# Cross-attention block with an int8-emulating FFN on one core: int8 rounding in both FFN stages, a reordered down projection, a reordered end of the input projection, and text denominators of the last two groups on TensorE

## The reference

```python
def _act_fake_quant(x, clip_factor):
    scale = sigmoid(clip_factor) * max(abs(x)) / 127
    return clip(round(x / scale), -128, 127) * scale      # one scale for the tensor
def _weight_fake_quant(w): ...                            # the same with one scale per row
x = x + xattn(layernorm(x), ctx, Wq, bq, Wk, bk, Wv, bv, Wo, bo)
xq = _act_fake_quant(layernorm(x), clip_x)
h = _act_fake_quant(silu(xq @ wq(w_gate).T) * (xq @ wq(w_up).T), clip_down)
x = x + h @ wq(w_down).T
# mask: 768 image tokens attend within three blocks of 256; 256 text tokens
# attend to all image tokens and causally to text
```

## Time and profile before

| | us |
|---|---|
| median of 3 runs | 1235.87 (1234.25 to 1235.88) |
| the profiled execution, its own time | 1234.68 |
| its span, first to last instruction | 1233.0 |

### The profile page before, as it was taken

The page is one execution under the profiler, slowest core; times in us unless marked ns, Lnnn a source line. Parts: engine busy times, 40 slices in busy tenths (PEclk is TensorE's granted clock), DMA queues, the critical chain, the costliest instruction groups (busy, mean ns, idle before and its releaser), DMA issues. The chain is left out here.

```text
span 1233.0 us, 18417 instructions
## 1 busy us (share of the span) xinstructions
PE 1070.3 (87%) x6494; PEld 704.9 (57%) x6518; DVE 793.9 (64%) x1340; ACT 518.9 (42%) x885; POOL 657.9 (53%) x359
## 2 busy tenths in 40 slices
PE   5999999999079899999999997059994999996866
PEld 4888888888056566666666653036662444443322
DVE  4666555564077577777777750219987678878975
ACT  3332222232006577667767776102221565544432
POOL 2543344553506889999999999224442121000635
PEclk8999999999558899999999999569997999998988
DMA  6987777766598968678868400585994551102485
GB/s 214 308 258 257 236 221 239 261 195 200 133 192 180 235 147 188 154 176 184 192 145 184 101 24 28 184 213 167 269 277 130 172 208 35 35 1 69 139 321 205
DMA packets 128699, 217.99 MB, mean 177 GB/s; under 512 B 29175, under 2 KB 54519, under 8 KB 127416
## 3 DMA queue, kind: packets, MB, share of 16 engines
q1 hardware_dynamic: 128632, 217.11, 62.7%
HBM read 134.76 MB, written 77.74 MB: 172 GB/s over the span
## 5 line engine op out<-in xcount | busy, mean ns | idle before, releaser
L618 ACT ACTIVATE a_probs<-a_st 128x512 f32<-128x512 f32 (+2 forms) x512 | 233.6, 535 | 128.1 <-PE a_st L733 97.7
L579 POOL TENSOR_TENSOR a_prob_sums<-a_probs 128x2048 f32<-128x2048 f32 x48 | 220.1, 4585 | 52.6 <-ACT a_probs L618 43.5
L658 DVE TENSOR_REDUCE a_max<-a_work 128x2 f32<-128x512 f32 x192 | 123.0, 684 | 59.3 <-PE a_work L704 59.1
L733 PE MATMUL a_st<-a_q_stack,a_k_stack 97*128 97x512 f32 x384 | 147.0, 426 | 8.3 <-DMA a_q_stack<-a_max_rows 4.5
L704 PE MATMUL a_work<-a_k_stack,a_q_stack 96*128 96x256 f32 x384 | 85.5, 318 | 38.8 <-DMA a_q_stack<-q_split 38.8
L709 PE MATMUL a_work<-a_k_stack,a_q_stack 96*128 96x512 f32 (+1 forms) x256 | 115.1, 464 | 0.0
L1303 POOL TENSOR_TENSOR d_out<-d_out,kept_ffn_x 128x512 f32<-128x512 f32 x32 | 49.5, 1579 | 121.9 <-DVE d_out L1340 121.9
L655 DVE CUSTOM_DVE_ANT_0 a_masked_scores<-a_work,kept_mask 128x384 f32<-128x384 f32 (+1 forms) x128 | 79.5, 621 | 53.2 <-PE a_work L709 53.0
L704 PEld LDWEIGHTS a_work<-a_k_stack,a_q_stack 96*128 96x128 f32 x384 | 69.9, 204 | 60.5 <-DMA a_q_stack<-q_split 39.5
L658 DVE TENSOR_REDUCE a_max_parts<-a_work 128x1 f32<-128x512 f32 x128 | 88.0, 688 | 25.0 <-PE a_work L709 21.1
L223 POOL TENSOR_SCALAR p_x<-p_x,p_neg_mean,p_rstd 128x512 f32<-128x512 f32 x32 | 28.1, 892 | 122.7 <-DVE p_rstd L328 122.7
(11 more groups left out here) (173 smaller groups left out, 2319.6 us busy)
## 6 DMA issues: line engine op xcount, KB each, us to landing
a_k_stack<-k_split SPq DMA_DIRECT2D x48, 512.0 KB, 8.3
a_q_stack<-q_split SPq DMA_DIRECT2D x48, 512.0 KB, 14.3
kept_ffn_x<-x_scratch SPq DMA_DIRECT2D x14, 1024.0 KB, 7.3
p_c<-in_ctx_dram SPq DMA_DIRECT2D x8, 1024.0 KB, 8.9
p_x<-in_x_dram SPq DMA_DIRECT2D x8, 1024.0 KB, 11.0
v_scratch<-p_v_stage SPq DMA_DIRECT2D x16, 512.0 KB, 9.2
k_split<-p_stage_hi SPq DMA_DIRECT2D x16, 512.0 KB, 4.1
k_split<-p_stage_lo SPq DMA_DIRECT2D x16, 512.0 KB, 5.3
```

The lines of the kernel that those rows point to most:

```text
L579: pool.tensor_tensor(PP[u % 2][:], PR[2 * c % 4][:], PR[(2 * c + 1) % 4][:], ALU.add).then_inc(paired, 1)
L618: act.activation(PR[kt % 4][:, j, 0:w], STB[:, n % NST, 0:w], ACT.Exp, scale=SCALE).then_inc(edone, 1)
L658: dve.tensor_reduce(out, src, AX.X, ALU.max).then_inc(wfree, 1)
L733: op = pe.matmul(out.rearrange("p (c t) -> p c t", t=SIT), keys, q, start=True, stop=True)
```

## The change

Four things are changed.

**Projection.** In the last two steps the four parts of `ffn_rows` stand between the four value tiles instead of the four key tiles. POOL does `quantise_ffn` of step 6 ahead of the layer norm of chunk 7. SP stores the quantised piece, and in the last step also the row scales, ahead of the query tiles.

**Attention.** In the last two groups (`i >= FOLDED`, 14 and 15) POOL folds nothing. PE multiplies the text columns of each pair by ones, and those of slots 6 and 7 straight from `PR`.

**gate_up and down, quantising.** One DVE pass multiplies by the inverse scale and writes int8 (which rounds and clips); ACT copies int8 to bf16. In `down` the int8 pieces go to one buffer `HI` of one chunk.

**down.** The loops are written out. The order of chunks is 6, 7, 2 to 5, 0, 1, so the spilled chunks are read back after the first and second. From chunk 1 on PE has the four token tiles outside and the k rows inside. The last chunk's residual is added by DVE tile by tile, and its output is stored in four pieces of 256 KB.

```diff
@@ project, SP, step()
+                def ffn_store():
+                    s.reach(sp, fq, n + 1)
+                    d = gu_q[u].rearrange("(b p j) n -> b p j n", p=FP, j=FJ)[b]
+                    sp.dma_start(d, FQ[:]).then_inc(fst, 16)
+                    sp.dma_start(d_q.rearrange("(s p) n -> s p n", p=DP)[n], DQ).then_inc(fst, 16)
                 for i in range(4):
+                    if tail and i == 2:
+                        ffn_store()
+                        if final:
+                            ffn_scales()
                     item = KEY + 2 * i if i < 2 else query(final) + 2 * (i - 2)
                     s.reach(sp, free, NB + at(n) + item + 2)
...
-                s.reach(sp, fq, n + 1)
-                d = gu_q[u].rearrange("(b p j) n -> b p j n", p=FP, j=FJ)[b]
...
+                if not tail:
+                    ffn_store()
                 if not final:
                     s.reach(sp, fst, 32 * (n + 2))
                     ffn_load(n + 1, 1 - u, b + u)
@@ project, POOL
+            quantise_ffn(NCH - 2)
             norm(1, NCH)
-            quantise_ffn(NCH - 2)
             quantise_ffn(NCH - 1)
@@ project, DVE, step(b, u, final, tail=False)
                     dve.tensor_tensor(VST[t // 2][:, t % 2, :], bank(u, VALUE + t), BV[:], ALU.add).then_inc(free, 1)
+                    if tail:
+                        ffn_rows(n, t)
...
                     staged(u, n, KEY + j, j, 0, 1, KT + j)
-                    ffn_rows(n, j)
+                    if not tail:
+                        ffn_rows(n, j)
@@ attend
+        FOLDED = NGRP - 2
...
-                if c:
+                if c and i < FOLDED:
                     text = PP[u % 2][:, :, SIT:]
...
-                pool.wait_ge(cutd, 2 * i + n + 1)
-                pool.tensor_tensor(text, text, probs, ALU.add).then_inc(folded, 1)
+                if i < FOLDED:
+                    pool.wait_ge(cutd, 2 * i + n + 1)
+                    pool.tensor_tensor(text, text, probs, ALU.add).then_inc(folded, 1)
...
+                if i >= FOLDED and not wi:
+                    op = denominators(TB, p, slice(0, wt))
                 op.then_inc(pvdone, 1)
...
                         pe.wait_ge(paired, 3 * i + kt // 2 + 1)
+                        if i >= FOLDED:
+                            denominators(TB, PP[(3 * i + kt // 2) % 2], slice(SIT, 512))
                         denominators(IB, PP[(3 * i + kt // 2) % 2], slice(0, SIT)).then_inc(iden, 1)
-                    if kt == NKT - 1:
+                    if kt == NKT - 1 and i < FOLDED:
@@ gate_up
-                act.activation(XQ[u][:], X[u][:], ACT.Copy, bias=-MAGIC).then_inc(xq, 1)
+                act.activation(XQ[u][:], XI[u][:], ACT.Copy).then_inc(xq, 1)
...
-                dve.tensor_scalar(X[u][:], X[u][:], F.ix[:, 0:1], QMAX, ALU.mult, ALU.min).then_inc(p1, 1)
-                dve.wait_ge(p1, n + 1)
-                dve.tensor_scalar(X[u][:], X[u][:], -QMAX - 1.0, MAGIC, ALU.max, ALU.add).then_inc(p2, 1)
+                dve.tensor_scalar(XI[u][:], X[u][:], F.ix[:, 0:1], None, ALU.mult).then_inc(rounded, 1)
@@ down
+ORDER = tuple(range(RES, NCH)) + tuple(range(2, RES)) + (0, 1)
+        HI = s.sb("hi", [P, IT, CH], I8)
...
+                sp.wait_ge(rounded, NG * (u + 1))
                 sp.dma_start(F.h[:, u], spill[u].rearrange("p (t q) -> p t q", t=IT)).then_inc(back[u], 16)
+            for n in range(LAST):
+                sp.wait_ge(added, TT * (n + 1))
+                sp.dma_start(rows(out, n), OUT[n % 2][:]).then_inc(stored[n % 2], 16)
+                if n + 2 < NCH:
+                    load(n + 2)
+            for t in range(TT):
+                sp.wait_ge(added, TT * LAST + t + 1)
+                sp.dma_start(rows(out, LAST)[:, t, :], OUT[1][:, t, :]).then_inc(stored[1], 16)
...
+            def quantise(n):
+                if n >= RES:
+                    dve.wait_ge(back[n - RES], 16)
+                for gi, (a, b) in enumerate(GROUPS):
+                    if n:
+                        dve.wait_ge(hq, NG * (n - 1) + gi + 1)
+                    dve.tensor_scalar(HI[:, a:b, :], F.h[:, n % RES, a:b, :], IH[:, 0:1], None, ALU.mult).then_inc(rounded, 1)
...
+                    dve.tensor_tensor(OUT[u][:, t, :], BK[:, u, t, :], F.sd[:], ALU.mult).then_inc(scaled, 1)
+                    if n == LAST:
...
+                        dve.tensor_tensor(OUT[u][:, t, :], OUT[u][:, t, :], X[u][:, t, :], ALU.add).then_inc(added, 1)
...
+            for k in range(IT):
+                for t in range(TT):
+                    tile(0, k, t)
+            for n in range(1, NCH):
+                for t in range(TT):
+                    for k in range(IT):
+                        tile(n, k, t)
```

More of the change, by code:

```diff
@@ L167, in _, with ffn_scales @@
             ffn_load(0, 0, 0)
+            def ffn_scales():
+                with nc.allow_non_contiguous_dma(reason="the scales of the rows, four to a line"):
+                    for u in range(2):
+                        sp.dma_start(gu_scales[u].rearrange("(b p j) -> p b j", p=FP, j=FJ), FS[0:FP, u::2, 0:FJ])\
+                          .then_inc(fsc, 16)
+                    sp.dma_start(d_scales.rearrange("(s p) -> p s", p=DP), FS[0:DP, :, FJ]).then_inc(fsc, 16)
             def step(b, u, tail, final):
@@ L202, in _ @@
                 sp.wait_ge(q, 16 * (NCH + 1))
-            with nc.allow_non_contiguous_dma(reason="the scales of the rows, four to a line"):
-                for u in range(2):
-                    sp.dma_start(gu_scales[u].rearrange("(b p j) -> p b j", p=FP, j=FJ), FS[0:FP, u::2, 0:FJ]).then_inc(fsc, 16)
-                sp.dma_start(d_scales.rearrange("(s p) -> p s", p=DP), FS[0:DP, :, FJ]).then_inc(fsc, 16)
             sp.wait_ge(fst, 32 * (NCH + 1))
@@ L1306, in _ @@
         @blk.scalar
         def _(act):
-            act.sem_inc(full, 2 * TT)
-            def step(n, u, slot):
-                act.wait_ge(full, TT * (n + 1))
+            for n in range(NCH):
+                if n >= 2:
+                    act.wait_ge(full, TT * (n - 1))
                 for gi, (a, b) in enumerate(GROUPS):
-                    act.wait_ge(p2, NG * n + gi + 1)
-                    act.activation(HQ[u][:, a:b, :], F.h[:, slot, a:b, :], ACT.Copy, bias=-MAGIC).then_inc(hq, 1)
```

141 lines of the change are left out of this document (59 added, 82 removed).

## The result

The changed kernel takes 1221.26 us (median of 4 runs, 1219.58 to 1222.71) against 1235.88 (1234.25 to 1236.03) beside it: ratio 0.9884, 95% interval 0.9867 to 0.9901. It is faster by 14.6 us (1.2%), not by the 35 forecast; 1221 lies above the range of 1190 to 1207.

What follows compares the result with a forecast made beforehand. It took PE to bound the projection, POOL attention, PE gate_up (first chunk exposed) and DVE down. Savings of 0 + 9.8 + 1.2 + 24.0 = 35.0 us from 1234.68 gave 1199.7 us, range 1190 to 1207.

Steps and rivals of the forecast that it cites:

- The wait put into step 6: Projection: DVE waits for the weight piece until 254.9, PE is held 5.8 us, then 2.4 lost to slow clock.
- Nothing else in step 6 comes too late: Projection: beyond that wait nothing is late; POOL's rounding runs from 261 to 275, step 6 is 8.2 us later in all.
- In step 7 PE does not wait: Projection: DVE waits again, but PE wants its bank at about 296.3 and value tile 1 frees it at 295.9.
- The end of the stage: Projection: ends at 326.4 to 326.8 against 326.3, term 0; query stores landing behind the scales add under 6.0 us.
- the 0.5 that the forecast itself allowed: Projection: POOL's last rounding ends at 312.5 instead of 312.0.
- Rival 3: Projection: scales and query stores hinder each other, or the slow clock lasts longer: +4 to +6 us, 1204; chance 0.15.
- the split: Attention: 9.8 us saved, about 3.1 in each of the last two groups and 3.6 at the end.
- The mis-sized term: Attention: a group falls from POOL's 24.3 us to ACT's 21.2, saving about 3.1; PE is not the bound.
- The term of 1.2: gate_up: one of two quantising passes goes in the exposed first chunk, saving 1.2 us.
- its terms: Down: 1.2 us earlier start, 17.5 from chunks paced by PE, 5.3 from the shorter end; 24.0 saved in all.
- Rivals 2 and 4: gate_up and down: int8 pass takes 2.28 us per 2048 elements (1202, chance 0.15), or 5.5 (1273, chance 0.03).
- the window of 9.50 us: Down: one steady chunk with DVE 9.43 of 9.50 us busy, read as DVE setting the rate before the change.

Runs made afterwards that it cites:

- g_only: Kernel before with only the int8 pass of gate_up added: median 1234.45 us, ratio 0.9997 to the kernel before.
- sp_order: Changed kernel with DVE's and POOL's projection of before, keeping only SP's new store order: ratio 0.9789 to the kernel before.
- scales_early: Changed kernel with the projection of before, but all three scale stores ahead of the last step's first query store: ratio 0.9681 to the kernel before.
- scales_split_end: Changed kernel with the projection of before, scales of pieces 0 to 6 stored in step 6, piece 7's at the very end: one run, 1202.87 us.
- down_scales_early: Changed kernel with the projection of before, only the down scales stored ahead of the last step's query stores: one run, 1196.44 us.
- p_only: Kernel before with only the projection part of the change: median 1253.02 us, ratio 1.0134 to the kernel before.
- pool_order: Changed kernel with POOL's layer norm of chunk 7 ahead of the rounding of piece 6 again: ratio 0.9873 to the kernel before.

## Why the prediction was wrong, point by point

- **The wait put into step 6** held: DVE idle 15.08 us, PE 6.17 for 5.8, slow clock behind it (granted clock 0.50 from 258.20 to 263.90, with matmul rows of 0.63 us for 0.39 at 1.00).
- **"Nothing else in step 6 comes too late"** is the step that failed. I followed value tile 1 and POOL, and not the rest of DVE's queue behind the hold: the norm of chunk 7 and four key tiles. The norm took from 263.39 to 275.07, and from 251.21 to 255.59 before; most of the 7.3 us more are the two rows above. For down the prediction reckoned with stalls beside POOL, and did not ask whether POOL's edit makes such a pair here. Price: the second gap of PE (4.79 us) and its slow clock (0.50 from 276.00 to 281.00), the load of piece 7 8.5 us later than forecast. Nor would the old order of POOL have saved the forecast: then POOL rounds piece 6 some 10 us later (271.45 for the 261 forecast), and the load goes out at 291.1 all the same.
- **"In step 7 PE does not wait"** fell with it: 1.48 us here, 6.2 to 9.45 in the variants. The load itself took 11.3 us and not 9.2, beside the query stores. Together the rounding of piece 7 starts at 309.55, not at 298.9.
- **The end of the stage.** The prediction took 0 for the query stores behind the scales, with a bound of 6.0; it is 6.3. From the issue of the last scales to the end of the stage it takes 17.2 us (326.63 to 343.80) for 10.8 before: 3.4 to issue the four stores, 2.9 more to land. The bound was the number to choose. The rule of the Trainium skill that the prediction weighed ("DMA: Bandwidth & Descriptors", Queues, rings and completion order), that an increment lands only after every earlier write of that engine, fits the stores' late landing; these runs don't test it, since the stores' own packets are slow too (20 GB/s above). The 10.7 of the late rounding and these 6.3, with the 0.5 that the forecast itself allowed, are the 17.5. Rival 3 had the 6.3 at +4 to +6; the larger share, 10.7, was in no rival.
- **Attention.** The sum was near (-6.3 for -9.8; over fifteen profiles of kernels with this part the stage is 446.3 on average, 6.8 less than in four without), but partly by luck, since the split was wrong: 0.4 per group for 3.1, 6.7 at the end for 3.6. The mis-sized term is the group, 21.2 from ACT's own times with PE called no bound. PE is busy 22.69 of 23.20 us in group 14 (from 730.10) and 20.40 of 23.19 in group 15, ACT 15.71 and 16.52, and in group 15 ACT and PE wait for each other at nearly every slot (0.53 to 1.51 us and 0.28 to 0.50). The trace before held the answer, its copies of groups 14 and 15 being 23.5 apart.
- **gate_up.** The first matmul comes 1.2 us earlier, as forecast (8.9 us into the stage for 10.2), but the low clock level lasted longer behind it, and the profiled stage won nothing. Windows of PE from the first matmul to the end of the low level, before and after (the fourth column is the clock):

```profile
957.80:960.60 2.80, 2.80 (x7) 0.50 1.14 305
```

```profile
968.60:974.10 5.50, 5.49 (x13) 0.50 1.21 302
```

  Over sixteen profiles with the int8 pass the stage takes 172.1 on average (171.5 to 172.8), in four without 173.6 (172.8 to 174.1). The term of 1.2 fits the averages and can't be seen in one pair of runs; the times don't show it either (g_only: 0.9987 to 1.0006, at most 1.6 us).
- **Down** was right in its terms: 78.0 us of chunks for 77.8, an end of 3.9 for 4.8, the start 2.2 earlier for 1.2 (the combined scale is now computed behind the first rounding). Rivals 2 and 4 are out: the int8 pass takes 1.28. Beside POOL it costs more: DVE is busy 9.50 us of the 9.50 from 1148.50 to 1158.00, and still in time. One reading was loose: the window of 9.50 us that was to show DVE's rate before is one in which PE was full too (9.45). The pace that DVE set is seen in the chunks behind it, which begin 11.87 us apart (1159.17, 1171.04 and 1182.91).
- **Output**: +0.7 us, in most kernels with the attention part (168.9 on average against 168.2); not explained.
- **The chances** do not fit together: those of the four rivals, the forecast, no change and the mixtures add up to 1.15, not to 1.

## What to carry to other kernels

An operation that is moved to an earlier place in a queue and waits there for a DMA stops everything behind it; follow that queue to its end, and the next round of the loop that asks for the same DMA, before giving the move a price of 0. Ask of each element engine what will now run beside it: the norm of one chunk took 4.4 us, or 11.7 beside POOL's rounding. The wait to be shortened at the end of a stage should first be asked what it consists of: here 8.5 of 9.7 us passed with no byte moving. Putting the cause earlier won 6.5 us, where putting it ahead of the large stores (sp_order) had cost 9.3.

## What the runs showed of the hardware

- Small stores: behind the last packet of 512 runs of 4 bytes and 704 of 16 no traffic for 8.5 us (kernel before); stores queued behind them move at 20 GB/s for 5 us and land 11.0 us after issue instead of 2.8 (scales_early). 64 runs of 4 bytes with 88 of 16 are waited for 6.3 us (scales_split_end), 704 runs of 16 bytes alone 2.8 (down_scales_early).
- Two DVE operations on 128x4 elements take 4.61 and 2.80 us beside POOL's rounding of 88x2048 and 64x1408 elements (changed kernel, p_only), and 0.17 and 0.16 without it (kernel before, pool_order).
- DVE from f32 to int8 in SBUF: 1.28 us for 2048 elements, as for f32 output; beside POOL's adds three pieces (5632 elements) take 6.17 that take 3.41 alone.
- The low clock level behind a stage border ended at different times for the same work: 2.8 and 5.5 us behind the first matmul of gate_up, which moves a stage by up to 1.4 us.
